# First score pass of a causal attention: the mask goes from a table read by VectorE into PSUM by TensorE

## What is computed

```python
scores = einsum('bhqd,bhkd->bhqk', rope(q), rope(k)) / sqrt(8)
scores = where(causal, scores, -inf)
out    = softmax(scores) @ v @ W_o.T
```

## Time and profile before

| | |
|---|---|
| median of 3 runs | 624.34 us (624.0 to 624.88) |
| the profiled execution | 620.97 us |
| its span, first to last instruction | 619.2 us |
| granted TensorE clock, mean over the span | 0.857 of full |
| PE / DVE / ACT / POOL busy | 77% / 66% / 45% / 32% of the span |
| the attention loop | about 309 to 514 us of the span |

### The profile page before, as it was taken

The page is one execution under the profiler, slowest core; times in us unless marked ns, Lnnn a source line. Parts: engine busy times, 40 slices in busy tenths (PEclk is TensorE's granted clock), DMA queues, the critical chain, the costliest instruction groups (busy, mean ns, idle before and its releaser), DMA issues.

```text
span 619.2 us, 10103 instructions
## 1 busy us (share of the span) xinstructions
PE 479.0 (77%) x3167; PEld 283.4 (46%) x3167; DVE 410.3 (66%) x1363; ACT 278.0 (45%) x510; POOL 197.7 (32%) x254
## 2 busy tenths in 40 slices
PE   4697779886989999995589994998599786009990
PEld 4554567765634444442334442344245235009990
DVE  4788668996456767677787893788488804305543
ACT  2477876642235454532225681476357471002330
POOL 4300059995105544445500120031000000453443
PEclk9888899996599999999756996599779898558996
DMA  9500000001500000002860035006200000022014
GB/s 361 142 1 1 0 2 2 2 0 35 244 1 0 1 2 0 0 1 70 210 130 2 3 105 103 2 4 173 34 3 3 2 2 1 31 86 76 32 36 148
DMA packets 25083, 31.75 MB, mean 51 GB/s; under 512 B 2444, under 2 KB 22860, under 8 KB 24508
## 3 DMA queue, kind: packets, MB, share of 16 engines
q1 hardware_dynamic: 23784, 28.52, 16.4%
q0 software_dynamic: 1248, 2.59, 1.3%
HBM read 19.42 MB, written 11.48 MB: 50 GB/s over the span
## 4 chain that ended last, share of the span: by engine, by line
PE 52%; DVE 18%; issue 8%; ACT 7%; DMA 5%; POOL 5%; SPq 5%; DVEq 0%; ACTq 0%; POOLq 0%
PE ps L1664 5%; PE ps L1547 5%; PE ps L1551 4%; PE ps L1535 4%; DVE moe L1151 3%; PE ps L1748 3%; PE ps L1619 3%; PE ps L1570 3%; DVE rows L386 2%; POOL slots_x L512 2%; PE ps L1759 2%; PE ps L1650 2%; SPq L312 2%; PE ps L1352 2%; DMA arena<-arena 2%
## 5 line engine op out<-in xcount | busy, mean ns | idle before, releaser
L1151 DVE CUSTOM_DVE_ANT_0 moe<-ps,const 128x512 bf16<-128x512 f32 (+3 forms) x256 | 113.0, 487 | 25.9 <-PE ps L1619 24.8
L701 ACT ACTIVATE arena<-ps 128x256 f32<-128x256 f32 (+3 forms) x128 | 86.4, 702 | 66.6 <-PE ps L1650 65.7
L1619 PE MATMUL ps<-arena 48*128 48x128 bf16 (+3 forms) x256 | 61.1, 346 | 15.3 <-DVE arena L1151 13.9
L1645 PE MATMUL ps<-bconst 64*128 64x64 bf16 x512 | 48.6, 203 | 17.3 <-DMA arena<-arena 15.6
L461 POOL TENSOR_TENSOR arena<-arena 128x512 f32<-128x512 f32 x30 | 38.1, 1270 | 68.4 <-DVE arena L1053 68.2
L1650 PE MATMUL ps<-arena 51*128 51x128 bf16 (+3 forms) x256 | 57.0, 328 | 0.0
L1664 PE MATMUL ps<-arena 128*32 128x512 f32 (+3 forms) x512 | 55.2, 507 | 0.9 <-ACT arena L701 0.6
L379 POOL TENSOR_SCALAR rs<-mv 128x4 f32<-128x4 f32 x20 | 5.3, 264 | 139.7 <-DVE mv L372 139.2
L1619 PEld LDWEIGHTS ps<-arena 48*128 48x128 bf16 x256 | 17.2, 98 | 68.5 <-DVE arena L1151 42.8
L1645 PEld LDWEIGHTS ps<-bconst 64*128 64x128 bf16 x512 | 31.6, 102 | 32.1 <-DMA arena<-arena 17.5
L1044 DVE SCALAR_TENSOR_TENSOR arena<-ps,arena 128x512 f32<-128x512 f32 x32 | 22.1, 692 | 27.7 <-ACT arena L677 27.7
(11 more groups left out here) (242 smaller groups left out, 1111.2 us busy)
## 6 DMA issues: line engine op xcount, KB each, us to landing
qk_parts<-arena SPq DMA_DIRECT2D x48, 128.0 KB, 2.3
arena<-qk_parts SPq DMA_DIRECT2D x16, 288.0 KB, 6.1
arena<-moe_in SPq DMA_DIRECT2D x1, 4100.0 KB, 14.0
moe<-moe_in SPq DMA_DIRECT2D x1, 1936.0 KB, 14.1
arena<-qk_parts SPq DMA_DIRECT2D x16, 96.0 KB, 2.2
slots_x<-zeros SPq DMA_DIRECT2D x1, 1518.0 KB, 20.5
arena<-slots_x SPq DMA_DIRECT2D x3, 396.0 KB, 4.3
const<-const_in SPq DMA_DIRECT2D x1, 1067.0 KB, 8.6
```

Source lines behind the costliest of these rows:

```text
L701: act.activation(pt[:, u % 4, :, 0:n], ps[:, 4 + 2 * k:6 + 2 * k, 0:n], ACT.Exp, scale=ATT_SCALE).then_inc(sem("probs"), 1)
L1151: v.tensor_tensor_reduce(out=junk[:, done % 2, 0:n], in0=ps[:, k, col:col + n], in1=w["mask"][:, (3 - qt) * P:4 * P], scale=1.0, scalar=3 ...
L1619: mm = pe.matmul(ps[:, k, col:col + n], qaug[lo:lo + KR, b % 2, 2 * g + j // 2, qt * P:(qt + 1) * P], kaug[lo:lo + KR, b % 2, 2 * g + j // ...
L1645: pe.matmul(ps[:, bank, HALF * qh:HALF * (qh + 1)], w["causal"][lo:lo + HALF, qh * P:(qh + 1) * P], w["half"][lo:lo + HALF, :], start=(qh ...
```

## The change

The table `mask` and the scrap tile `junk` go away; a constant `before` (128 x 256, bf16) comes in. TensorE first writes the mask of a unit's diagonal blocks with two matmuls, 64 columns wide for a unit with one tile and 128 wide for one with two, on the same 64 partitions as the unit's heads; the scores are then accumulated on them. VectorE takes a plain maximum along the free axis. The two heads of a 256 + 256 unit are taken by one instruction, so there are 14 a step, not 16, and no accumulator to read.

```diff
-              ("mask", 512), ("segment", NT * E1), ...
+              ("segment", NT * E1), ...
-BPACK = [("identb", 128), ("causal", 256), ("half", 64), ("sel0", 1024)]
+BPACK = [("identb", 128), ("causal", 256), ("before", 256), ("half", 64), ("sel0", 1024)]
...
-            [[(1, 0), (1, 2)]],
-            [[(1, 1), (1, 3)]],
+            [[(1, (0, 2))]],
+            [[(1, (1, 3))]],
...
-                        ring.append((("mx", it + 2, n), ("mx", 16 * (it + 2) + maxima_done[n + 1])))
+                        ring.append((("mx", it + 2, n), ("mx", MAXIMA * (it + 2) + maxima_done[n + 1])))
...
-                for c, (qt, j) in enumerate(units[u]):
-                    n = P * (qt + 1)
-                    done = 16 * s + maxima_done[u] + c
-                    if done >= 2:
-                        v.wait_ge(sem("mx"), done - 1)
-                    v.tensor_tensor_reduce(out=junk[:, done % 2, 0:n], in0=ps[:, k, col:col + n],
-                                           in1=w["mask"][:, (3 - qt) * P:4 * P], scale=1.0, scalar=3 * NEG,
-                                           op0=ALU.add, op1=ALU.max, accum_out=mx[:, s % 2, qt, j:j + 1])\
+                for qt, js in units[u]:
+                    n = P * (qt + 1) * len(js)
+                    src = ps[:, k, col:col + n].rearrange("p (j t) -> p j t", j=len(js))
+                    v.tensor_reduce(mx[:, s % 2, qt, js[0]:js[-1] + 1:2].unsqueeze(2), src, AX_X, ALU.max)\
                         .then_inc(sem("mx"), 1)
                     col += n
...
                 k = ring_bank("mx", s, i)
+                parts = [(qt, j) for qt, js in units[i] for j in js]
+                lo = HALF * (parts[0][1] % 2)
+                step = P * (parts[-1][0] + 1)
+                for kh in range(2):
+                    diagonal = ps[:, k, 512 - len(parts) * step:512].rearrange("p (j t) -> p j t", j=len(parts))\
+                        [:, :, step - P + HALF * kh:step - P + HALF * (kh + 1)]
+                    half = w["half"][lo:lo + HALF, :].unsqueeze(1).to_broadcast([HALF, len(parts), HALF])
+                    pe.matmul(diagonal, w["before"][lo:lo + HALF, kh * P:(kh + 1) * P],
+                              half, start=(kh == 0), stop=True, skip_group_check=True)
...
                     mm = pe.matmul(ps[:, k, col:col + n],
                                    qaug[lo:lo + KR, b % 2, 2 * g + j // 2, qt * P:(qt + 1) * P],
-                                   kaug[lo:lo + KR, b % 2, 2 * g + j // 2, 0:n], start=True, stop=True)
+                                   kaug[lo:lo + KR, b % 2, 2 * g + j // 2, 0:n], start=False, stop=True,
+                                   skip_group_check=True)
```

More of the change, by code:

```diff
@@ L53 @@
     "const": [("ident", 128), ("tri", 128), ("after", 128), ("cos", 512), ("sin", 512), ("iota", 8),
-              ("mask", 512), ("segment", NT * E1), ("full", NT), ("block", NBLK), ("number", NT), ("spare", NBLK)],
+              ("segment", NT * E1), ("full", NT), ("block", NBLK), ("number", NT), ("spare", NBLK)],
 }
-BPACK = [("identb", 128), ("causal", 256), ("half", 64), ("sel0", 1024)]
+BPACK = [("identb", 128), ("causal", 256), ("before", 256), ("half", 64), ("sel0", 1024)]
 def offsets(fields):
@@ L189, in adaln_kernel @@
         qk = used.take(2 * S).rearrange("p (k t) -> p k t", k=2)
-        junk = used.take(2 * S, BF16).rearrange("p (k t) -> p k t", k=2)
         pc = ar.take(6 * S, BF16).rearrange("p (a i t) -> p a i t", a=2, i=3)
@@ L237, in adaln_kernel @@
         FIRST_PASS = [
[L238 to L241, removed]
-            [[(1, 0), (1, 2)]],
-            [[(1, 1), (1, 3)]],
-            [[(3, 2)], [(3, 3)]],
-            [[(2, 2), (0, 2)], [(2, 3), (0, 3)]],
+            [[(3, (0,))]],
+            [[(3, (1,))]],
+            [[(2, (0,)), (0, (0,))]],
+            [[(2, (1,)), (0, (1,))]],
+            [[(1, (0, 2))]],
+            [[(1, (1, 3))]],
+            [[(3, (2,))], [(3, (3,))]],
+            [[(2, (2,)), (0, (2,))], [(2, (3,)), (0, (3,))]],
         ]
@@ L254, in adaln_kernel @@
                 maxima_done.append(maxima_done[-1] + len(parts))
+        MAXIMA = maxima_done[-1]
         def ring_projection(b, j):
@@ L1160, in max_parts @@
                 if step == 0:
-                    v.wait_ge(sem("mx"), 16 * (s + 1))
+                    v.wait_ge(sem("mx"), MAXIMA * (s + 1))
                 else:
@@ L1614, in scores @@
                 k = ring_bank("mx", s, i)
+                parts = [(qt, j) for qt, js in units[i] for j in js]
[7 more added lines that the diff above has]
+                              half, start=(kh == 0), stop=True, skip_group_check=True)
                 col = 0
-                for qt, j in units[i]:
+                for qt, j in parts:
                     n = P * (qt + 1)
-                    lo = HALF * (j % 2)
                     mm = pe.matmul(ps[:, k, col:col + n],
                                    qaug[lo:lo + KR, b % 2, 2 * g + j // 2, qt * P:(qt + 1) * P],
-                                   kaug[lo:lo + KR, b % 2, 2 * g + j // 2, 0:n], start=True, stop=True)
+                                   kaug[lo:lo + KR, b % 2, 2 * g + j // 2, 0:n], start=False, stop=True,
+                                   skip_group_check=True)
                     col += n
@@ L1774, in shape_constants @@
     sin = np.sin(ang)[:, d // 2].T * np.where(d % 2 == 0, -1.0, 1.0)[:, None]
-    mask = np.zeros((P, 4 * P), np.float32)
-    mask[:, 3 * P:4 * P] = np.where(k[None, :] > k[:, None], NEG, 0.0)
     const = {
         "ident": np.eye(P), "tri": k[:, None] <= k[None, :], "after": k[:, None] > k[None, :],
-        "cos": cos, "sin": sin, "iota": np.broadcast_to(8.0 - np.arange(8), (P, 8)), "mask": mask,
+        "cos": cos, "sin": sin, "iota": np.broadcast_to(8.0 - np.arange(8), (P, 8)),
         "segment": np.broadcast_to(np.arange(NT * E1) % NT > 0, (P, NT * E1)),
@@ L1792, in shape_constants @@
         "causal": np.concatenate([np.where(k[None, :] > k[:, None] % HALF + HALF * qh, NEG, 0.0) for qh in range(2)],
+                                 axis=1),
+        "before": np.concatenate([np.where(k[:, None] % HALF + HALF * kh > k[None, :], NEG, 0.0) for kh in range(2)],
                                  axis=1),
```

## The result

The changed kernel takes 627.68 us (median of 10 runs, 623.88 to 631.58), the kernel before 623.81 us (10 runs): a ratio of 1.0086, 95% interval 1.0056 to 1.0115. The two medians alone would give 1.0062. But three of the ten runs of before are the earlier ones that the prediction started from; the other seven average 622.51 us, the ten of the changed kernel 627.87, and that is 1.0086. So the kernel became slower, by 5.4 and by 7.1 us; the prediction had +6.0. The ratios leave out executions that are more than 1.5% above the fastest of their kernel (four of twelve in e1, two of six in e4, one of twelve in e7); the medians do not.

The account below looks back on a forecast made before the run. PE alone was taken to bound half-clock stretches, a PE and DVE cycle `it` = 11. Stretch terms of 6.65 us, less 0.6 for absent reads, were taken as +6.0 on 624.34: 630.3 us, range 624.0 to 634.5.

Parts of the forecast that it names:

- the 0.6 for the reads: Accumulator reads absent on VectorE: 0.01 us each, some 60 on the chain, taken off the sum.
- The price of a mask: On PE, a one-tile unit's masks cost 0.06 us (half clock 0.12), a two-tile unit's 0.12 (0.22), weight loads included.
- The new masks lie on that same half, so they count whole: In PE's slots: the array half carrying the unit sets the length; 0.78 us a step at full clock, 1.46 at half.
- VectorE's gain: Where DVE leads: 0.18 us a step from the merged units in slots 4 and 5, plus 0.14.
- `it` = 0, half clock, PE: +1.5: First attention stretch: chain on PE alone at half clock, masks add 1.5 us.
- `it` = 11: slot 3 0.12, less 0.18: Full-clock cycle of PE and DVE: masks charged in slot 3 only, less VectorE's saving; -0.05 us.
- `it` = 1: +0.3: Slots 0 and 1 at half clock, 2 and 3 at full: 0.24 + 0.24, less 0.18 us.
- DMA wait near 7 us: Sign in the changed profile: PE's wait for the DMA chain falls from 8.26 to near 7 us.
- the +0.5 for `it` = 3 and 7: Only slots 0 to 2, before the DMA chain starts, count: 2 x 0.24 us.
- A: Rival: masks go into PE's holes, only DVE's gain is seen; 622.4 us, chance 0.05.
- C: Rival: a plain maximum does not overlap the next instruction, DVE grows 0.9 us a step; 635.5 us, chance 0.09.
- B: Rival: denser masks raise PE's clock sooner in `it` = 0, 5, 6, 9, 10, 13; 619.8 us, chance 0.08 in full.

Follow-up runs that it names:

- e1: Kernel before plus the change's masks on TensorE, VectorE's fused instructions kept: 629.65 us, 1.0072 of before.
- e4: Kernel before, second-pass masks of one head written three times in slots 0 to 5, on the half carrying the first-pass unit: 1.0180 of before.
- e7: Kernel before with 28 more matmuls on TensorE in the DMA waits ahead of `it` = 5 and 9: 621.43 us, 0.9985 of before.
- c2: Second run of the changed kernel without its masks, 14 plain maxima, first pass left unmasked: 0.9994 of before.
- c1: The changed kernel measured again, nothing altered: 628.32 us, 1.0115 of before.
- e5: Changed kernel with each mask matmul issued twice: 633.40 us, 1.0199 of before.
- e3: Kernel before, second-pass masks of one head written three times in slots 0 to 5, on the half without a first-pass unit: 1.0018 of before.
- e8: Changed kernel without its masks and with 16 plain maxima instead of 14, first pass left unmasked: 0.9995 of before.
- e2: Changed kernel without its masks, 14 plain maxima, first pass left unmasked, first run: 0.9972 of before.
- e6: Changed kernel with masks and 16 plain maxima instead of 14, the 256 + 256 units taken apart: 1.0113 of before.

## Why the prediction was right, point by point

The forecast was +6.0 us; measured were +5.4 and +7.1. The direction, the mechanism and the size hold. The forecast time of 630.3 us came out at 627.68, as it starts from 624.34 and the runs of before beside the changed kernel average 622.51. Its terms, at clocks equal to 0.01 where the rows have a pair:

| stretch | forecast | measured | pair (clock) |
|---|---|---|---|
| `it` = 0 | +1.5 | +0.7 | 11.04, 11.75 (0.50) |
| `it` = 1 | +0.3 | +0.7 | 8.30, 9.00 (0.94, 0.93) |
| `it` = 2 | +0.8 | +0.7 | 12.12, 12.84 (1.00) |
| `it` = 5 | +0.7 | +0.65 | 14.73, 15.38 (0.50) |
| `it` = 6 | +0.9 | +0.9 | 13.99 in c2, which has no masks, 14.86 (both 0.85) |
| `it` = 9 | +0.7 | +0.8 | 13.55, 14.36 in c1 (0.75, 0.74) |
| `it` = 10 | +0.4 | +0.75 | 9.48, 10.23 (0.82, 0.81) |
| `it` = 11 | -0.05 | +0.05 | 8.42, 8.47 (1.00) |
| `it` = 12 | +0.5 | +0.2 | 9.96, 10.14 (1.00) |

These nine add up to 5.45 us against 5.75 forecast. Where two clocks differ by 0.01, some 0.1 us of the difference is the clock's (an estimate from `it` = 10: 9.48 us at 0.82 before, 8.29 at 0.95 in e7). The rest of the forecast, 0.90 us less the 0.6 for the reads, lies in stretches without a clean pair. That the sum fits so well is in part luck: `it` = 0 and 12 were put too high by 1.1 us together, `it` = 1 and 10 too low by 0.75.

- **The price of a mask, right.** 0.06 us for 128 columns, weight load included, and 0.78 a step at full clock: `it` = 2 shows 0.72, 0.75 (e1) and another 0.78 (e5, beside c1).
- **"The new masks lie on that same half, so they count whole", right.** Shown by e3 beside e4.
- **VectorE's gain, 0.32 us a step, right but for the size:** 0.39 in `it` = 11. The 0.60 us at 512 columns are as forecast. e8 puts 0.10 of the 0.39 on the merging and 0.29 on the plain maximum, where I had 0.18 and 0.14: the two parts were mis-sized in opposite directions.
- **"`it` = 0, half clock, PE: +1.5", mis-sized.** The masks alone cost 1.2 there (e1) and VectorE gave 0.5 back (e2), which I had put at nothing. 1.17 - 0.48 = 0.69, and 0.71 was measured. Slots 0 and 1 pass through VectorE even at half clock, as the chain over the whole of `it` = 0 shows; the earlier trace rows begin behind them.
- **"`it` = 11: slot 3 0.12, less 0.18", right in size, wrong in kind.** Only slot 3 was to be charged. But the masks made TensorE's whole round (all its work of one `it`), 8.47 us, longer than VectorE's, so a second bound stood just behind the first. Masks alone give +0.26, plain maxima alone -0.39; their sum, 8.29, was not reached.
- **"`it` = 1: +0.3", mis-sized, probably for the same reason.** Its masks were charged in four slots, less VectorE's gain. With masks TensorE's round takes 8.46 us there even at full clock (c1), where before it took 8.30 with a little half clock in it.
- **"DMA wait near 7 us", not confirmed.** Ahead of `it` = 5 it is 7.63 us after (7.86 in c1) against 8.26 before, but ahead of `it` = 9 it is 8.00 (7.66 in c1) against 7.29: the two together are 15.6 us before and after. So the +0.5 for `it` = 3 and 7 is neither shown nor refuted.
- **The other signs.** VectorE's busy time fell by 6.3 us (forecast 3 to 5), and `it` = 0 came to 11.75 us at 0.50, not 12.5.
- **Rivals.** A fell with e1, C with e2 and the 0.60 us. B did not decide: every version with masks in the first pass is slower than before. In single stretches something like it is to be seen: the clock of `it` = 0 was 0.50 in one profile of the changed kernel and 0.59 in the other, whose `it` = 0 took 10.50 us, less than the 11.04 of before; in e6 it was 0.61. In e1 and e5, also with the masks, it was 0.50, and so it was in the seven profiles without them. Over all executions no rise shows: the median of the mean clocks is 0.853 in c1 against 0.857 before, and 0.856 in e1 against 0.854. The rule that activity releases the throttle (the Trainium skill, "TensorE: Matmul & The Clock Gate", What's actually happening) is not enough to forecast it: in e5 TensorE was busy for all the 16.23 us of `it` = 9, and the clock stayed at 0.50.

Left open: how much of the difference between 5.4 and 7.1 us is the clock, and whether the masks move it at all.

## What to carry to other kernels

Work moved from an engine that leads by a few per cent to the one just behind it can gain at most about that lead, and is charged wherever the other one led already. Here VectorE's half alone gave 0.39 us in `it` = 11, 0.48 in `it` = 0 and nothing in `it` = 2; TensorE's half alone took 0.26, 1.17 and 0.75 us there. Before moving work, measure in every stretch how long each of the two engines needs for one step, and where a matmul uses half of the array's rows, charge it only if its half carries the slot.

## What the runs showed of the hardware

- Matmuls of 51 and 64 rows on the two halves of the array proceed side by side, a later one of the free half starting before an earlier one of the loaded half (in the slot shown above, line 1650 at 472.20, before the second mask of line 1618 at 472.25, which precedes it in the program); 24 more a step on the free half lengthened `it` = 2 and 11 by 0.00 us.
- A reduction of 512 columns from PSUM frees VectorE after 0.60 us though it lasts 0.68 to 0.69.
- The clock is not led by how busy PE is alone: it stayed at 0.50 through 16.23 us with PE busy all of them (e5, `it` = 9). Filling the DMA wait with 6 us of work kept it at 1.00 there, but it was 0.50 again as `it` = 5 began (e7).
